# Decoder block, last MLP: which engine rounds the high part of the inner activations

## The reference, cut to what matters

```python
W1 = _compose_weight(fc1_logits, fc1_A, fc1_B)          # (256, 1024)
W2 = _compose_weight(fc2_logits, fc2_A, fc2_B)          # (1024, 256)
h = jax.nn.gelu(jnp.einsum('bsd,df->bsf', x, W1))       # tanh form
return jnp.einsum('bsf,fd->bsd', h, W2)
...
x = _layernorm(x + _L0_ffn_ref(x, ...), axis=-1)
```

## Time and profile before

| | before |
|---|---|
| three runs | 1019.98, 1020.62, 1022.62 us; median 1020.62 |
| the profiled execution | 1020.84 us, of it the span of the trace 1018.9 us |
| busy over the span | PE 95%, PEld 82%, DVE 67%, ACT 55%, POOL 47% |
| busy from 912 to 938.4 us (f_h of groups 0 and 1) | PE 25.40 of 26.40 us, DVE 18.70, ACT 14.06, POOL 17.23 |
| busy from 949.8 to 963.6 us (f_h of group 2) | PE 12.72 of 13.80 us, DVE 9.30, ACT 5.08, POOL 7.74 |
| busy from 975 to 990 us (f_h of group 3) | PE 13.03 of 15.00 us, DVE 8.61, ACT 4.18, POOL 8.75; granted clock 0.89 |

### The profile page before, as it was taken

How to read it: one execution, slowest core, us unless ns; L and a number is a source line. 1 busy time by engine, 2 the same in 40 slices (tenths; PEclk the granted TensorE clock), 3 DMA queues, 4 the chain that set the end, 5 groups by cost and what they waited for, 6 DMA issues and landing times.

```text
span 1018.9 us, 21835 instructions
## 1 busy us (share of the span) xinstructions
PE 970.1 (95%) x8589; PEld 833.2 (82%) x8589; DVE 684.7 (67%) x1457; ACT 564.0 (55%) x1342; POOL 478.1 (47%) x376
## 2 busy tenths in 40 slices
PE   5669999999999999999999999999999989999997
PEld 4457888888888888888888888888888769998887
DVE  6767677676766767686677768676431876767543
ACT  3437576666757667665856766675724443454210
POOL 3609154737745472765546277552416230007440
PEclk9678999999999999999999999999999999999999
DMA  6021000000210000021000002000155894740001
GB/s 198 20 64 42 2 17 1 2 17 1 84 42 17 2 1 17 1 84 42 18 1 1 18 1 85 1 18 32 31 108 139 156 190 93 162 71 1 22 22 42
DMA packets 71534, 47.57 MB, mean 47 GB/s; under 512 B 44464, under 2 KB 68112, under 8 KB 71440
## 3 DMA queue, kind: packets, MB, share of 16 engines
q1 hardware_dynamic: 71439, 46.27, 18.7%
HBM read 44.16 MB, written 2.10 MB: 45 GB/s over the span
## 4 chain that ended last, share of the span: by engine, by line
PE 85%; DVE 6%; SPq 2%; issue 2%; ACT 2%; POOL 1%; DMA 1%; POOLq 0%; DVEq 0%; ACTq 0%
PE F L1395 18%; PE F L1245 17%; PE A L1245 15%; PE A L1512 4%; PE A L1669 4%; PE A L1342 4%; PE A L1300 3%; PE F L1258 2%; PE A L1258 2%; PE A L1359 2%; PE F L1238 2%; PE A L1642 1%; PE A L1238 1%; PE A L1333 1%; PE A L1316 1%
## 5 line engine op out<-in xcount | busy, mean ns | idle before, releaser
L1245 PE MATMUL F<-xt,w 128*128 128x512 f32 x864 | 219.9, 403 | 4.6 <-ACT scratch L1229 3.9
L1245 PEld LDWEIGHTS F<-xt,w 128*128 128x128 f32 x864 | 158.8, 189 | 45.9 <-ACT scratch L1229 7.0
L427 POOL TENSOR_TENSOR ht<-scratch,ht 128x512 fp32r<-128x512 f32 x128 | 175.5, 1390 | 41.6 <-ACT ht L1070 40.2
L1395 PE MATMUL F<-w,ht 128*128 128x256 f32 x1536 | 190.7, 283 | 1.9 <-POOL ht L427 1.9
L1395 PEld LDWEIGHTS F<-w,ht 128*128 128x128 f32 x1536 | 184.1, 189 | 7.8 <-issue 4.6
L415 POOL TENSOR_TENSOR rstd<-var,minus_half 128x4 f32<-128x4 f32 x32 | 37.6, 1175 | 194.6 <-DVE var L547 194.3
L1067 ACT ACTIVATE scratch<-F,b_now 128x512 f32<-128x512 f32 x128 | 87.5, 684 | 36.6 <-POOL ht L427 19.3
L1245 PE MATMUL A<-wa,xt 128*128 128x512 f32 x384 | 92.6, 397 | 0.0
L422 POOL TENSOR_TENSOR x<-x,vec_f 128x1024 f32<-128x1024 f32 x16 | 37.9, 2367 | 102.0 <-DVE scratch L567 102.0
L1245 PEld LDWEIGHTS A<-wa,xt 128*128 128x128 f32 x384 | 71.3, 188 | 16.5 <-issue 0.2
L1070 ACT ACTIVATE ht<-scratch 128x512 fp32r<-128x512 f32 x128 | 81.0, 633 | 4.1
(11 more groups left out here) (214 smaller groups left out, 2007.8 us busy)
## 6 DMA issues: line engine op xcount, KB each, us to landing
raw_f<-in_L_attn_W_dram SPq DMA_DIRECT2D x8, 1024.0 KB, 5.6
scratch<-in_L_ffn_fc_B_dram SPq DMA_DIRECT2D x32, 256.0 KB, 4.8
scratch<-in_L_ffn_fc_A_dram SPq DMA_DIRECT2D x32, 256.0 KB, 4.1
x<-in_x_dram SPq DMA_DIRECT2D x4, 512.0 KB, 5.0
raw_f<-in_L_ffn_fc_A_dram SPq DMA_DIRECT2D x32, 64.0 KB, 4.0
scratch<-in_x_dram SPq DMA_DIRECT2D x1, 2048.0 KB, 11.5
raw_f<-in_L_ffn_fc_B_dram SPq DMA_DIRECT2D x32, 64.0 KB, 3.6
out_dram<-x SPq DMA_DIRECT2D x3, 512.0 KB, 3.0
```

What stands on the lines that cost most here:

```text
L427: pool.tensor_tensor(ht[:, 1, m, :], hf[:, m % 2, :], ht[:, 0, m, :].bitcast(F32), ALU.subtract).then_inc(h_lo, 1)
L1245: last = pe.matmul(out, lhs(a, c), rhs(b, c), start=k == 0, stop=k == len(total) - 1)
L1395: last = pe.matmul(F[:, t % 2, 0:D], ht[:, a, c, P * t:P * t + P], w2[:, b, c, :], start=k == 0, stop=k == len(passes) - 1)
```

## The change

VectorE's casts of the high parts are taken out, and with them `f_h_hi_parts`. ScalarE, behind each gelu, waits for that gelu's own semaphore and then does the rounding as a Copy activation from `hf` to the same place, and signals `f_h_hi` in VectorE's stead. The other operations and their order on each engine stay.

```diff
@@ VectorE
-            def f_h_hi_parts(p, chunks):
-                for m in chunks:
-                    dve.wait_ge(f_gelu, FC * p + m + 1)
-                    dve.tensor_copy(f_ht(p, 0, m), hf[:, m % 2, :]).then_inc(f_h_hi, 1)
-
             f_xt_lo_part(0)
             for k in range(4):
                 composed(*w2_part(k), 4 + k)
             for p in range(ITEMS):
-                f_h_hi_parts(p, range(4))
                 if p + 1 < ITEMS:
                     f_xt_lo_part(p + 1)
-                f_h_hi_parts(p, range(4, FC))
                 if p:
                     for t in range(TILES):
                         f_add(p - 1, t)
@@ ScalarE
                     act.activation(hf[:, m % 2, :], F[:, m % 2, :], ACT.Gelu_apprx_tanh).then_inc(f_gelu, 1)
+                    act.wait_ge(f_gelu, FC * p + m + 1)
+                    act.activation(f_ht(p, 0, m), hf[:, m % 2, :], ACT.Copy).then_inc(f_h_hi, 1)
```

## The result

The changed kernel takes 1014.53 us (median of four runs, 1013.97 to 1016.37) against 1021.13 us (1019.98 to 1022.62), a ratio of 0.9938 with a 95% interval of 0.9919 to 0.9956. Beside the last experiments it was timed once more: 1014.74 us, ratio 0.9956 (0.994 to 0.9973). The profiled execution took 1013.97 us, with a span of 1011.9.

A forecast was written before the change was run, and what follows sets the result against it. In the last MLP, GpSimd's subtraction plus the unhidden part of VectorE's cast was taken as the bound, 1.65 us a chunk. Gains 0.7 + 1.6 + 3.5 = 5.8 us from 1020.84 give 1015.0 us, range 1013.7 to 1017.2.

The forecast's parts named there:

- TensorE becomes the bound: Last MLP's inner chunks: new ScalarE-GpSimd loop takes 1.36 us a chunk, below TensorE's 1.402; first stretch 21.4 instead of 22.1.
- floor: TensorE's own time in the last MLP: 1.402 us a chunk, 0.87 us for the next group's eight transposes.
- f_h(2): Eight inner chunks of token group 2, last MLP: 13.79 us before, forecast 12.2, gain 1.6.
- f_h(3): Eight inner chunks of token group 3, last MLP: 14.97 us before, forecast 11.45, gain 3.5.
- The sum: Gains of the last MLP's three stretches: 0.7 + 1.6 + 3.5 = 5.8 us, giving 1015.0 us.
- The clock: Group 3's inner products: TensorE falls to half clock after idling 1.97 us, costing 1.63 us; forecast full after the change.
- ScalarE's slower copy doesn't matter: Rounding in the last MLP: ScalarE's copy takes 0.63 us against VectorE's 0.415, yet the move was forecast to gain.
- If subtractions took 1.56 us ... a chunk 1.5: Rival for the last MLP's new loop: slower than TensorE, gain about 4.2, 1016.6 us; chance 0.10.
- VectorE beside GpSimd: Norm's scalings beside GpSimd's first subtractions: no effect taken as likelier; rival of turn-taking gives 1016.0 us, chance 0.15.
- my upper bound: Scalings and subtractions beside the norm take turns, each subtraction 0.35 us late; gain 4.8 in all, 1016.0 us.
- The two engines take turns, and the loop is GpSimd plus the unhidden part of the cast: Last MLP before the change: 1.65 us a chunk, subtraction 1.28 to 1.29 plus 0.37 waiting for VectorE's cast.
- Four of the like form (L558) took 1.67 alone: Price of four VectorE operations without GpSimd, compared with L567's 4.77 and 5.94 us beside four subtractions.

The follow-up runs named there:

- the last experiments: Four kernels timed together, kernel before at 1019.56 us: the change again, and three with four gelu-result slots and early table load; medians 1012.60 to 1014.74 us.
- e_reorder: Kernel before, casts still on VectorE, those of chunks 0 and 1 moved ahead of the norm's scaling; 1015.81 us beside 1018.87.
- e_filler: Kernel before with eight unread transposes added ahead of chunk 4 of group 3; 1017.64 us beside 1018.87.
- e_two_copies: Changed kernel with every ScalarE copy done twice, the first result unused; 1019.85 us, beside 1019.85 for the kernel before.
- e_beside: Changed kernel plus an unused VectorE copy for each chunk of groups 0 and 1, awaited by nobody; 1014.85 us, beside 1019.85 for the kernel before.
- e_four_slots: Kernel before, casts on VectorE, with four slots instead of two for the gelu's result; 1013.38 us beside 1019.85.

## Why the prediction was right, point by point

- **TensorE becomes the bound.** Held: floor 1.402 us a chunk, gelus at 1.40; 21.45 us where 21.4 was forecast. One term of the floor reads differently than the prediction says: from the transposes to the next product it is 0.79 us (953.65 to 954.44), not 0.87, and the four chunks behind take 5.70 us, not 5.61; the sum is the same.
- **f_h(2)**: 12.10, forecast 12.2. **f_h(3)**: 11.47, forecast 11.45; its chunk 4 started 5.78 us into the stretch (977.36), forecast 5.85. The reasoning by queue positions (GpSimd behind the power, roundings ahead of chunk 4) held; e_reorder, by the same steps, was 12.79 and 12.74 for 12.9 and 12.9. The tenth too much in f_h(2): gelu 4 ended 9.15 us into the stretch (it started sooner behind the roundings than I had it), not at 9.32, and no matmul waited for it.
- **The sum**: 5.8 us forecast, 5.84 in the stretches. The 1015.0 us was 0.5 over the measured 1014.53, and the profiled span (1011.9 for 1013.1) falls short by the 1.1 us that lie ahead of the last MLP, which I could not know and which other executions do not have.
- **The clock** as a consequence of idling: shown by e_filler, which adds work and gains 1.2 us. The prediction's 1.6 was 0.4 too much; that 0.4 was the loop's, which the change removes as well, so the gain of 3.5 us in f_h(3) did not hang on the split.
- **ScalarE's slower copy doesn't matter** against TensorE's pace: with 0.63 us for the copy TensorE stays the bound. The room is small, since half a microsecond more a chunk takes the whole gain (e_two_copies); from which length on the copy begins to cost, no run shows. The rule of the Trainium skill that the prediction cites (ScalarE: Activation LUTs, "Rules for kernel authors") names relu, max, min, add and mul and compares rates per element; carried over to this copy, it would have given the wrong sign.
- **"If subtractions took 1.56 us ... a chunk 1.5"** is a slip in a rival: GpSimd alone would then need 1.56 us a chunk. It did not come to this; the subtractions of the changed kernel last 1.29 to 1.34 us.
- **VectorE beside GpSimd: the forecast value was right by luck, its reason wrong.** I took no effect as likelier, since a scaling takes 0.345 us for 256 columns, where the cast that is held took 0.415 for 512. The scalings did collide (1.36 us each). The stretches stayed short because of who pays: the subtractions took 1.34 instead of 1.29, where my upper bound had each 0.35 late. The bound took L567's 5.94 us for four, 1.49 each, for full turns, though those rows already showed GpSimd losing only 0.2. The Trainium skill, SBUF — State Buffer, "SBUF: two separate sides", lets whichever starts first keep the shared pair for its whole instruction; e_beside agrees for VectorE (0.43 us when it starts first, 0.71 when second), while GpSimd as the loser is late by 0.18 us, less than the 0.43 of the copy; only behind back-to-back casts (e_four_slots, 1.74 us) does it lose 0.45. Why only that much, no run here tells.
- **"The two engines take turns, and the loop is GpSimd plus the unhidden part of the cast": incomplete.** e_four_slots has the same casts, and behind the table load's pause TensorE never waits. The turns alone bring 1.65 us in some phases and 1.45 in others; that TensorE pays for the 1.65, and that it lasts, takes the two slots as well: a gelu then waits for a subtraction, so the cast behind it always falls 0.36 us into the next subtraction, where it is held to the end. Take either away, and the stretch is 21.45 us. Likewise the norm's place cost 5.2 us only because two slots passed the delay on to the gelus. So rounding on ScalarE is one of two cures, and the slots are the other. Together they give no more than the slots alone, which are 0.3 us better in f_h(3) than the change.
- **"Four of the like form (L558) took 1.67 alone": misread.** They did not run alone. GpSimd's power, on 4 columns, ran beside them from 313.28 us on:

```profile
313.28 1.18 POOL L415 TENSOR_TENSOR rstd<-var,minus_half 128x4 f32<-128x4 f32 x1 [10.85 <-DVE var L547]
```

The upper bound is not changed by it, but the 1.67 us is no price of the four operations without GpSimd.

## What to carry to other kernels

Write the loop out in queue positions, with each handoff from a row: a chain over four engines came out within 0.1 us a stretch, and within 0.2 in e_reorder. If a helper engine's loop is slower than TensorE, ask first whether more slots in the buffer between them remove the wait; here two more gave what moving 32 operations gave, because the helper can catch up during the output products. And price a pause of TensorE together with the clock that it may cost.

## What was not expected of the hardware

- A VectorE copy or cast (128x512 fp32, buffer to buffer) and a GpSimd subtraction share unequally: the cast is held for up to 0.8 us (0.42 to 1.22), the subtraction for 0.05 us beside scalings (1.29 to 1.34), 0.18 beside single copies (1.30 to 1.48) and 0.45 beside casts back to back (1.29 to 1.74, e_four_slots).
- The scaling with two per-partition scalars on 256 columns takes part in this (1.36 us instead of 0.345), although undisturbed it takes 0.345 us for 256 columns where the cast takes 0.415 for 512.
- After 1.08 and 1.10 us of idling TensorE kept 2.4 GHz, after 1.97 us it fell to 1.2 GHz; eight transposes in the gap of f_h(3) were enough to keep it. The granted clock was 0.50 from 984 to 987 us and full again from 988, while TensorE worked without a pause from 982.76.
